# A DLRM interaction tower on one core, rewritten: unsplit fp32 vectors, products in 32x32 column tiles, four more tables looked up for half of the samples

## The reference

```python
# B = 512 samples, 32 fields, vectors of D = 256; tables of 1000, 1250 or 12500 rows, fp32
e = stack([tbl_f[ids[:, f]] for f in range(32)], axis=1)     # 512 x 32 x 256
z = einsum("bnd,bmd->bnm", e, e)[:, iu, ju]                  # 496 products of pairs, i < j
h = concatenate([z, dense_ctx], axis=1)                      # 512 x 512 (dense_ctx: 512 x 16)
h = maximum(h @ W_top1 + b_top1, 0)                          # 512 x 512
h = maximum(h @ W_top2 + b_top2, 0)                          # 512 x 256
y = h @ W_top3                                               # 512 x 1
```

## Time and profile before

| | us |
|---|---|
| median of 3 runs | 205.6 (204.4 to 206.85) |
| the profiled execution: its span; no other time of it is given | 231.3 |
| PE busy / PEld busy | 159.4 / 138.9 |
| DVE busy | 137.5 |
| ACT busy | 114.1 |
| POOL busy, 112 gathers of it | 113.2, 112.5 |
| first lookup matmul starts | 11.4 |
| last gather issued | 170.7 |

### The profile page before, as it was taken

The page is one execution under the profiler, slowest core; times in us unless marked ns, Lnnn a source line. Parts: engine busy times, 40 slices in busy tenths (PEclk is TensorE's granted clock), DMA queues, the critical chain, the costliest instruction groups (busy, mean ns, idle before and its releaser), DMA issues.

```text
span 231.3 us, 2991 instructions
## 1 busy us (share of the span) xinstructions
PE 159.4 (69%) x976; PEld 138.9 (60%) x976; DVE 137.5 (59%) x256; ACT 114.1 (49%) x198; POOL 113.2 (49%) x118
## 2 busy tenths in 40 slices
PE   0097497004997577584986775199769759969995
PEld 0075375003785466474976763098659749959994
DVE  0363564104898479999639566753878793793500
ACT  2111462005775759594543658181756944663521
POOL 1777777763787767377556676465730000000000
PEclk9999679655899999887699999569988988996799
DMA  2555555556995333223223233223220000000000
GB/s 67 173 177 176 183 191 181 191 182 189 269 317 165 89 96 91 71 79 102 72 90 103 82 91 92 78 71 101 82 77 0 0 1 3 0 0 0 3 0 0
DMA packets 10055, 22.76 MB, mean 98 GB/s; under 512 B 2647, under 2 KB 2775, under 8 KB 10044
## 3 DMA queue, kind: packets, MB, share of 16 engines
q0 software_dynamic: 5376, 14.69, 21.4%
q1 hardware_dynamic: 4408, 7.67, 10.2%
q10 hardware_dynamic: 260, 0.26, 0.4%
HBM read 22.61 MB, written 0.00 MB: 98 GB/s over the span
## 4 chain that ended last, share of the span: by engine, by line
PE 41%; DVE 21%; issue 18%; ACT 10%; another core or an unknown queue 5%; DMA 4%; DVEq 1%; ACTq 0%
PE dots_ps L516 10%; DVE xt L269 9%; PE xt_ps L535 8%; PE mlp_ps L563 8%; PE dots_ps L550 6%; ACT xt L378 5%; DVE pairs L290 5%; DVE summed L283 4%; DMA chunk_rows_sb<-chunk_rows 4%; PE xt_ps L563 3%; PE mlp_ps L575 2%; ACT kept L371 2%; DVE one_hot L315 1%; PE mlp_ps L557 1%
## 5 line engine op out<-in xcount | busy, mean ns | idle before, releaser
L257 POOL DMA_INDIRECT rows<-table,row_ids x112 | 112.5, 1005 | 57.7 <-issue 30.2
L269 DVE TENSOR_TENSOR xt<-xt_ps,xt 128x512 fp32r<-128x512 f32 x64 | 64.5, 1010 | 39.8 <-ACT xt L378 35.2
L378 ACT CAST xt<-xt_ps 128x512 fp32r<-128x512 f32 x64 | 60.9, 951 | 46.4 <-PE xt_ps L535 31.4
L550 PE MATMUL dots_ps<-xt 128*128 128x256 f32 x256 | 48.7, 324 | 10.2 <-DVE xt L269 5.3
L535 PE MATMUL xt_ps<-ident,rows 128*128 128x128 f32 x224 | 41.0, 305 | 12.6 <-DVE xt L269 12.0
L516 PE MATMUL dots_ps<-one_hot,high 125*128 125x512 f32 x64 | 24.3, 466 | 34.3 <-DVE low L320 27.9
L550 PEld LDWEIGHTS dots_ps<-xt 128*128 128x128 f32 x256 | 38.5, 214 | 13.2 <-issue 8.0
L535 PEld LDWEIGHTS xt_ps<-ident,rows 128*128 128x128 f32 x224 | 29.6, 156 | 18.6 <-DVE xt L269 14.3
L516 PEld LDWEIGHTS dots_ps<-one_hot,high 125*128 125x128 f32 x64 | 12.9, 221 | 38.1 <-issue 34.2
L563 PE MATMUL mlp_ps<-pairs,w_sb 128*128 (+1 forms) x208 | 31.1, 297 | 2.6 <-DVE pairs L290 2.6
L423 ACT CAST high<-small_sb 125x512 fp32r<-125x512 f32 x16 | 10.0, 627 | 42.1 <-issue 25.7
(11 more groups left out here) (30 smaller groups left out, 65.2 us busy)
## 6 DMA issues: line engine op xcount, KB each, us to landing
small_sb<-small_tables SPq DMA_DIRECT2D x16, 250.0 KB
w_sb<-w SPq DMA_DIRECT2D x8, 256.0 KB
rows<-table,row_ids POOLq DMA_INDIRECT x112
small_ids_sb<-small_ids SPq DMA_DIRECT2D x3, 250.0 KB
w_sb<-w SPq DMA_DIRECT2D x1, 512.0 KB
small_ids_sb<-small_ids ACTq DMA_DIRECT2D x1, 250.0 KB
ids_sb<-ids SPq DMA_DIRECT2D x1, 112.0 KB, 4.1
w1d_sb<-w1d SPq DMA_DIRECT2D x1, 32.0 KB
```

The lines of the kernel that those rows point to most:

```text
L257: nc.gpsimd.indirect_dma_start(rows[:, slot, :], None, table, bass.IndirectOffsetOnAxis(ap=row_ids[:, m * GATHERS + t:m * GATHERS + t + 1] ...
L269: nc.vector.tensor_tensor(to, fill_ps(n, u, fields), xt_fill(n, 0, u)[0], ALU.subtract).then_inc(b_ready, 1)
L378: nc.scalar.copy(to, fill_ps(n, u, fields)).then_inc(a_ready, 1)
L550: last = nc.tensor.matmul(dots_ps[h][:, g % HALF, :, :], x[:, 0, :], x, start=(c == 0), stop=(c == DC - 1))
```

## The change

The whole of `build_tower` is rewritten; the reference, the inputs and the output stay.

- **Vectors stay fp32.** `xt` holds each vector once; `take_b`, `take_aa`, `take_dots` and `summed` are gone. A fill is moved by one copy, ACT's for two fills in three and DVE's for the third (`by_dve`). The vectors from `kept` are one copy too, on ACT and DVE in turn.
- **Products in column tiles.** For each sample, `x` (128 x 32) is stationary and moving at once and writes 32 PSUM partitions; four samples use the four quadrants. That is 1024 fp32 matmuls of 32 by 32 (in the trace two instructions each, as every fp32 matmul) for the 256 before, called in 32 halves of a batch, `dots(half)`. Squares are moved straight from PSUM to `pairs`.
- **Gathers and lookups.** 104 gathers for 112: for the second half of the samples eight fields are looked up and 24 gathered. The four added lookups have 256 columns, 64 matmuls of `high` and 64 of `low`. The 1000 rows are padded to 1024, so that a table is 128 partitions by 8 chunks. One pair of banks takes all lookups, so a table waits until `kept` has been written from the one before (`found_kept`).
- **Dense features** stand in `pairs` at column 0 and go through layer 1; `dense_part` is gone. The row numbers come with the gather ids in one transfer.
- **Order.** 12 fp32 matmuls of the identity run ahead of the first lookup. Then the 16 pairs of chunks of the first four tables with 14 fills between them, then 15 rounds of three fills each with two `dots` halves (one ahead of the lookups and MLP pieces, one behind), lookups in the first six rounds, and the tail.

```diff
-LOOKED_UP = 4
+LOOKED_UP = 4, 8
+WARM_UP = 12
+EARLY = 14
+ROUND_FILLS = 3
+LEAD_DOTS = [[0], [2], [4], [6], [8], [10], [13], [15], [17], [19], [21], [23], [25], [27, 28]]
+TWOS_IN = [3, 3, 3, 3, 2, 2] + [0] * (ROUNDS - 6)
...
-        xt = sb("xt", [P, BATCHES, DC, 2, SAMPLES, N_FIELDS], F32R)
-        summed = sb("summed", [P, 2, UNIT * BATCH, P])
+        xt = sb("xt", [P, KEEP, DC, SAMPLES, N_FIELDS])
...
+            def take_xt(f):
+                if not by_dve(f):
+                    act.wait_ge(transposed, f + 1)
+                    nc.scalar.copy(*fill_parts(f)).then_inc(xt_act, 1)
...
             def look_up(two):
                 for i in range(2 * two, 2 * two + 2):
                     k, c = divmod(i, CHUNKS)
-                    if c == 0 and k >= 2:
-                        pe.wait_ge(found_kept, k - 1)
+                    if c == 0 and k:
+                        pe.wait_ge(found_kept, k)
...
-                for g in range(2 * u, 2 * u + 2):
-                    for c in range(DC):
-                        x = xt[:, n, c, :, g * GROUP:(g + 1) * GROUP, :].rearrange("d h s f -> d h (s f)")
-                        last = nc.tensor.matmul(dots_ps[h][:, g % HALF, :, :], x[:, 0, :], x,
-                                                start=(c == 0), stop=(c == DC - 1))
+                for g in groups:
+                    for c in range(DC):
+                        for s in range(GROUP):
+                            x = xt[:, n % KEEP, c, g * GROUP + s, :]
+                            done = nc.tensor.matmul(dots_ps[bank][Q * s:Q * (s + 1), u, g, :], x, x,
+                                                    start=(c == 0), stop=(c == DC - 1))
...
+            for _ in range(WARM_UP):
+                nc.tensor.matmul(xt_ps[0][:, 0:P], ident[:], ident[:], start=True, stop=True)
+            for two in range(FIRST_TWOS):
+                look_up(two)
+                for f in FILLS_BEHIND.get(two, ()):
+                    fill(f)
+            for r in range(ROUNDS):
+                for half in LEAD_DOTS[r]:
+                    dots(half)
+                for two in twos_in(r):
+                    look_up(two)
...
+                for half in TRAIL_DOTS[r]:
+                    dots(half)
+                for f in fills_in(r):
+                    fill(f)
...
-    chunks = 8
-    kr = n_rows // chunks
+    chunks = 8
+    kr = P
+    filled = [np.pad(tables[f], ((0, kr * chunks - n_rows), (0, 0))) for f in looked_up]
```

More of the change, by code:

```diff
@@ L166, in build_tower @@
         stored = sem("stored")
[L168 to L212, removed]
@@ new lines, in half_of, with first_fill, batch_fill, fill_gathers @@
+        def half_of(n):
+            return n // HALF_BATCHES
+        def first_fill(n):
+            return sum(FILLS[half_of(m)] for m in range(n))
+        def batch_fill(f):
+            n = next(m for m in range(NM) if f < first_fill(m + 1))
+            return n, f - first_fill(n)
+        def fill_gathers(f):
+            n, u = batch_fill(f)
+            first = sum(GATHERS[half_of(m)] for m in range(n))
+            return range(first + 2 * u, first + min(2 * u + 2, GATHERS[half_of(n)]))
@@ new lines, in fills_in, with dots_place, moves @@
+        def fills_in(r):
+            return range(EARLY + r * ROUND_FILLS, EARLY + (r + 1) * ROUND_FILLS)
+        def dots_place(n):
+            return (n // UNIT % 2, n % UNIT) if n < NM - 1 else (0, 0)
+        def moves(v, s, batches=range(UNIT)):
+            b, at = v // UNIT, s * Q + v % UNIT * UNIT * GROUPS
+            first, number = batches[0], len(batches)
+            bank, u = dots_place(v * UNIT + first)
+            for q in range(QUADS):
+                skip = int(q == 0)
+                to = pairs[Q * q:Q * (q + 1), b % 2, skip:, at + first * GROUPS:at + (first + number) * GROUPS]
+                source = dots_ps[bank][Q * s:Q * (s + 1), u:u + number, :, q * JJ + skip:(q + 1) * JJ]
+                yield to.rearrange("i j (u g) -> i j u g", g=GROUPS), source.rearrange("i u g j -> i j u g")
@@ L218, in _, with load_dense @@
             sp.dma_start(ids_sb[:], ids).then_inc(ids_in, 16)
[L219 to L224, removed]
+            def load_dense(b):
+                sp.dma_start(pairs[0:dense.shape[0], b % 2, 0, :],
+                             dense[:, b * BLOCK:(b + 1) * BLOCK]).then_inc(dense_in, 16)
@@ L249, in _ @@
             pool.wait_ge(ids_ready, 1)
[L252 to L256, removed]
+            for f in range(NF):
+                if fill_gathers(f)[-1] >= ROWS:
+                    pool.wait_ge(transposed, next(e for e in range(f) if fill_gathers(f)[-1] - ROWS in fill_gathers(e)) + 1)
+                for i in fill_gathers(f):
@@ L294, in step @@
[L294 to L305 removed]
+            nc.vector.tensor_tensor(row_ids[:], gather_ids[:, 0, :], gather_ids[:, 1, :], ALU.add).then_inc(ids_ready, 1)
@@ L555, in dense_part @@
-            def dense_part(b, n, banks, start=False):
-                return nc.tensor.matmul(banks[n], w1d_sb[:, n * P:(n + 1) * P],
-                                        dense_sb[:, bass.ds(b * BLOCK, BLOCK)], start=start, stop=not start)
-            def pairs_part(b, n, columns, banks, start=True, stop=False):
-                for j in columns:
-                    done = nc.tensor.matmul(banks[n], w1_sb[:, j, n * P:(n + 1) * P], pairs[:, b, j, :],
-                                            start=(start and j == 0), stop=(stop and j == JJ - 1))
-                return done
@@ L662, in _ @@
+            b = NB - 1
+            for half in (2 * NM - 2, 2 * NM - 1):
+                dots(half)
+            layer2_of(b - 1)
+            pairs_complete(b)
+            pe.wait_ge(h1_ready, N1 * b)
+            for k in range(N1 + 1):
                 if k < N1:
-                    pairs_part(last, k, range(JJ), last_l1_ps, start=False, stop=True).then_inc(l1_done, 1)
+                    layer1(b, k, range(JJ), last_l1_ps[k])
+                if k == 2:
+                    layer3(b - 1, l3_ps)
```

671 lines of the change are left out of this document (316 added, 355 removed).

## The result

| | before | after |
|---|---|---|
| median of the runs | 206.2 us (204.4 to 206.9, 4 runs) | 172.6 us (172.0 to 174.1, 4 runs) |
| ratio, 95% interval | | 0.842 (0.835 to 0.848) |
| profiled span | 231.3 | 170.9 |

The forecast was 174 us, with a range of 152 to 210. The profiled execution of the changed kernel spans 170.9 us and that run took 172.8: the span lies 2 us under the time, and no ratio as I had assumed lies between them.

The account below looks back on a forecast made before the run. PE was taken as the bound: its terms, from first lookup through products to tail, summed to 194.5 us on the profile's scale, times 0.889 gave 172.9, plus 1 for slow stretches 174 us; range 152 to 210.

Parts of the forecast that it names:

- a small price off by more than 10 ns: Sign of being wrong: the price of a small product matmul instruction on PE, taken as 0.028 us, misses by over 10 ns.
- a profile whose excess is not a ratio: Sign of being wrong: the profiled span's 25.7 us above the runs' median does not scale as a ratio.
- The products: PE term: 2048 instructions of 32 columns at 0.028 us, a quarter of the 128-column price, 57.3 us against 30.7.
- rival B: Gathers become the bound: product tiles overlap, 0.007 to 0.02 us an instruction, total 143 to 158 us; chance 0.25.
- The ratio of 0.889: Whole-kernel correction from profile to runs, 205.6 / 231.3, turning the sum of 194.5 into 172.9 us.
- The lookups: PE terms: first four tables 128 x 0.225 = 28.8 us, added four tables 128 x 0.12 = 15.4 us.
- A change of size: PE switching between 32 and 128 columns, 58 times: between 0 and 10 us, taken as 4.6.
- three stops: PE standing behind tables of the first stage for copies and hand-overs: 2.6 us each, 7.8 in all.
- A: The forecast case: PE sets the pace, a small instruction costs 20 to 40 ns, 158 to 195 us; chance 0.47.
- C: Rival: PE's issue of weight-load and matmul pairs bounds the products, slower; loses from 0.046 us a pair; chance 0.17.
- D: Rival: hand-overs bound; PE waits a further 2 to 3 us in each of 15 rounds, 206 us; chance 0.11.
- The rate of the tables: Table loading at 293 GB/s removes 19 us of PE's table waits; at 87 GB/s the waits stay.

Follow-up runs that it names:

- the tile-by-tile kernel: Changed kernel with the product loops reordered, eight matmuls in a row into one quadrant, then the next: 201.1 us, 0.970 of the kernel before.
- the second pair of banks: Changed kernel with a second pair of lookup banks for tables 1 and 3: 165.6 us, 0.808 of the kernel before by medians.
- the last two runs: Changed kernel with products in four runs of 32, 258.0 us; with two bank pairs and round 0 looking up first, 263.4; kernel before on that chip 235.2.
- the second trace of the kernel before: The kernel before, unchanged, profiled once more: spans 204.5 us, run took 206.3 us.
- the padded kernel: The kernel before with its four tables padded to 1024 rows, 128 partitions by 8, nothing else: 184.8 us, 0.896 of the kernel before.

## Why the prediction was right, and where it was not

The time is right within 1%, and that is luck: two of its steps are wrong, by 32 and by 22 us, in opposite directions. Both are among the signs by which I had said I would be wrong, a small price off by more than 10 ns and a profile whose excess is not a ratio.

**The products were mis-sized**: 57.3 us in the sum, 25.1 measured, 32 too much. I took a quarter of the 128-column price, which the tile-by-tile kernel confirms for one tile. Four quadrants in turn overlap and cost 0.012: this is rival B's price, to which I gave a chance of 0.25.

**The ratio of 0.889 was wrong**; it took off 21.6 us. The excess of the trace of 231.3 lay in waits of that one execution, all ahead of its last 42 us, while the terms that I read from single distances hold in any. Without the ratio and with my price I would have said 194.5. With the products as measured the sum is 194.5 - 32.2 = 162.3, against 170.9 in the trace: 8.6 short.

**The terms behind the 8.6.** The lookups took 51 us of PE for the 44.2 of the sum: the granted clock is 0.50 for 3.4 us from 20.1 and from 33.8 us and 0.51 from 57.6, each time 0.7 to 1.5 us after PE had stood for 2.1 to 2.6. The transposes took 25 for 22.9 and the MLP 39 for 37.7. A change of size costs 205 ns from a full matmul to a small one where 112 is usual, and 126 from a small one, which costs 12, to a full one: 0.2 a group and 6 in all for my 4.6. That is 0.1 us a change, less than the 0.17 of my upper end, and the trace doesn't show that it is a drain. Waits of 1.9 us for the last fill's copy and 1.0 for gathers stood nowhere in the sum. Against this the first lookup came at 7.1 for 8, three stops took 2.10 of idle time each for 2.6, the fourth 2.6 for 3.0, those of the half tables 1.18, 1.47 and nothing for 1.5 each, and the tail took some 2 us less. The last gather went out at 140.5 for 141.

**What bounds it**: PE, as forecast (A), but the rival's floor stands right beneath: B's gathers end 7 us ahead of PE, and the second pair of banks uses them up. C did not come as a price, since a pair of weight load and matmul follows in 0.007 at the median; what there is of it are 3.2 us of stops that I put down to instructions. In the last two runs a loss did come, in stops whose cause is open. D did not: ACT and DVE are busy 78 and 81 us, less than my 110 and 90, since ACT's copy to `xt` takes 0.59 and a move 0.26, not the 1.06 and 0.41 of the earlier trace rows.

**The rate of the tables** was a choice between two measured ones, 293 and 87 GB/s, made for the weights' 128 partitions; no row of the kernel before shows that the partitions set it. The runs bear the choice out: ACT's waits for tables are 34.9 us in 12 waits in the second trace of the kernel before, 3.3 us in one wait with 128 rows, and 5.0 us in the kernel after.

**Where the gain is**: 206 to 185 is the padding of the tables. 185 to 173 is the rewrite with the same 112 gathers. In the two traces 10 of these 12 us lie behind the start of the last transposes: from there to layer 2 of the third block PE needs 8.0 us in the padded kernel (155.1 to 163.1, with MLP pieces and a wait of 1.97 for a fill) and 2.2 in the rewritten one (152.6 to 154.8), and from layer 2 to the end 19.4 and 15.1. Which edit of the rewrite gives which part was not tried. 173.0 to 172.6 are the half tables.

## What to carry to other kernels

Look at the partition count of a transfer before anything else on the path it feeds: 125 for 128 cost 21 us here. Put small matmuls into the four column tiles in turn: the order of three loops was worth 28.5 us. When a time is made by scaling a trace, first see the same kernel's trace twice. A resource that a change saves (8 gathers) pays only after the next bound (the stops) is gone, so try such edits in pairs. Count an engine's instructions as well as its columns: with 128 small matmuls in a row for 64 the kernel was 8 us slower, and its trace has 6.4 us more of stops with no releaser.

## What the runs showed of the hardware that was not expected

- Matmuls of 128x32 by 32 columns, fp32, into four column tiles in turn start 7 ns apart at the median and cost 12 ns each over all, 11 without the stops; in one tile 31 at the median and 27 over all.
- Transfers of 250 KB over 125 partitions leave SP every 3.0 us beside the gathers in the kernel before (every 1.5 to 2.8 in the changed kernel with 125 rows), those of 256 KB over 128 every 0.5 in the same kernel with 128 rows (1.86 us for four).
- The page counts 6 `instruction` transfers of 16 KB for the 1952 instructions of PE in the kernel before, and 23 for 5744 in the kernel after. PE's 31 stops without a releaser, of 0.2 to 2.7 us, come where at least 114 of its last 150 matmul instructions were small, and 30 of them end 1.2 to 1.6 us after such a transfer has landed.
- On one chip PE stands 52 and 62 us with no releaser in all, and other engines wait for releasers that the profile can't name, as in the first trace of the kernel before.
